# A four-block kernel: the scan's last chunks in an order of their own, and the key weights brought forward in attention

## What is computed

```python
x = x + attn(layernorm(x), wq, wk, wv, wo)
x = x + ffn(layernorm(x), ...)
x = x + mixer(layernorm(x), in_proj_w, conv_w, ..., out_proj_w)
x = x + ffn(layernorm(x), ...)
# mixer, after projection, convolution and silu:
Y_diag = einsum('bcln,bcsn,bhcls,bcshp->bclhp', Cm, Bm, exp(segsum(A)), x)
Y_off  = einsum('bcln,bchpn,bhcl->bclhp', Cm, states, exp(A_cumsum))
y = Y_diag + Y_off + xs * D
g = y * silu(z)
g = g * rsqrt(mean(g * g) + 1e-5) * norm_w
out = g @ out_proj_w.T
```

## Time and profile before

| | us |
|---|---|
| median of 3 runs | 529.23 (528.64 to 529.54) |
| profiled execution | 529.58 |
| its span, first to last instruction | 527.8 |
| TensorE busy | 506.1 (96% of the span) |
| VectorE busy | 410.0 (78%) |
| ScalarE busy | 312.7 (59%) |
| GpSimd busy | 145.7 (28%) |
| mean granted TensorE clock, share of full speed | 0.997 |

### The profile page before, as it was taken

One profiled execution on the slowest core, in us unless ns is written; L12 is line 12 of the kernel. 1 busy time (PEld: TensorE's weight loads), 2 busy tenths in 40 slices (PEclk: granted clock), 3 DMA queues, 4 the chain that ended last, 5 costly groups with the idle time before them and its releaser, 6 DMA issues.

```text
span 527.8 us, 9002 instructions
## 1 busy us (share of the span) xinstructions
PE 506.1 (96%) x2939; PEld 427.1 (81%) x2939; DVE 410.0 (78%) x900; ACT 312.7 (59%) x783; POOL 145.7 (28%) x285
## 2 busy tenths in 40 slices
PE   5999999999999999999999999989988999999996
PEld 4778899999999987678888888758877768888884
DVE  5626567667675898899998999965886779899777
ACT  3656878688687754665443445998762355443342
POOL 2241425344243320110110302379434120020110
PEclk9999999999999999999999999999999999999999
DMA  7320100000001303000040000000000000000101
GB/s 281 105 95 1 36 7 2 2 0 2 2 2 25 131 2 140 6 1 0 1 140 1 2 0 1 1 1 2 0 2 0 1 1 1 1 0 1 40 2 40
DMA packets 5789, 14.23 MB, mean 27 GB/s; under 512 B 624, under 2 KB 2928, under 8 KB 5744
## 3 DMA queue, kind: packets, MB, share of 16 engines
q1 hardware_dynamic: 5744, 13.67, 7.4%
HBM read 12.62 MB, written 1.05 MB: 26 GB/s over the span
## 4 chain that ended last, share of the span: by engine, by line
PE 67%; DVE 19%; issue 6%; ACT 5%; POOL 2%; DMA 1%; DVEq 0%; ACTq 0%; POOLq 0%
PE psum L172 55%; PE psum L475 4%; DVE xs L1973 2%; PE psum L507 2%; DVE ln_stats L212 2%; DVE f_t L1296 1%; DVE xn L232 1%; PE psum L240 1%; DVE f_ch L1365 1%; DVE f_ch_hl L1379 1%; DVE xT_hl L254 1%; POOL ln_rstd L226 1%; DVE f_mix L1374 1%; ACT f_sil L1182 1%; PE psum L468 1%
## 5 line engine op out<-in xcount | busy, mean ns | idle before, releaser
L172 PE MATMUL psum<-xT_hl,ffn_w_hl 128*128 128x512 f32 x312 | 77.7, 396 | 0.9 <-ACT f_sil L1182 0.6
L172 PE MATMUL psum<-f_um,ffn_w_hl 128*128 128x512 f32 x288 | 72.9, 399 | 1.1 <-DVE f_t L1296 0.6
L172 PEld LDWEIGHTS psum<-xT_hl,ffn_w_hl 128*128 128x128 f32 x312 | 56.4, 189 | 13.3 <-DVE ffn_w_hl L897 1.4
L172 PEld LDWEIGHTS psum<-f_um,ffn_w_hl 128*128 128x128 f32 x288 | 53.1, 188 | 15.0 <-DVE f_um L1308 1.7
L1182 ACT ACTIVATE f_sil<-psum 128x512 f32<-128x512 f32 (+1 forms) x48 | 28.1, 596 | 48.8 <-PE psum L172 48.8
L1206 ACT ACTIVATE f_ch_hl<-f_ch 128x512 fp32r<-128x512 f32 x48 | 30.4, 632 | 42.2 <-DVE f_ch L1365 40.5
L172 PE MATMUL psum<-xT_hl,wq_hl 128*128 128x512 f32 x192 | 52.0, 407 | 0.6 <-ACT qT L574 0.6
L172 PE MATMUL psum<-wo_hl,oT_hl 128*128 128x256 f32 x384 | 50.8, 281 | 1.0 <-DVE oT_hl L707 0.6
L172 PEld LDWEIGHTS psum<-wo_hl,oT_hl 128*128 128x128 f32 x384 | 47.8, 188 | 3.7 <-DVE oT_hl L707 1.1
L574 ACT ACTIVATE qT<-psum 128x512 f32<-128x512 f32 x32 | 35.3, 1104 | 22.5 <-PE psum L172 22.4
L583 ACT ACTIVATE probs<-probs,small 120x66 f32<-120x66 f32 x120 | 39.8, 338 | 8.2 <-DVE small L684 8.2
(11 more groups left out here) (265 smaller groups left out, 1152.4 us busy)
## 6 DMA issues: line engine op xcount, KB each, us to landing
w_raw<-in_wq SPq DMA_DIRECT2D x4, 512.0 KB, 4.4
w_raw<-in_wo SPq DMA_DIRECT2D x4, 512.0 KB, 3.3
ffn_w_raw<-in_ffn SPq DMA_DIRECT2D x3, 576.0 KB, 4.9
ffn_w_raw_far<-in_ffn SPq DMA_DIRECT2D x3, 576.0 KB, 5.0
ssd_w_raw<-in_ssd SPq DMA_DIRECT2D x3, 512.0 KB, 5.4
x_resid<-in_x SPq DMA_DIRECT2D x2, 512.0 KB, 4.5
out_x<-x_resid SPq DMA_DIRECT2D x4, 256.0 KB, 2.1
w_raw<-in_wk SPq DMA_DIRECT2D x1, 512.0 KB, 6.6
```

What stands on the lines that cost most here:

```text
L172: i = e.matmul(dst, lhs(a), rhs(b), start=start and n == 0, stop=stop and n == len(TERMS) - 1, **kw)
```

## The change

In attention, SP transfers the identity alone (64 KB) behind x's first half, then wk, then x's second half; the other constants come last, and one unused constant is dropped. ACT splits wk in two halves ahead of the high part of half 0; DVE subtracts wk's first half right behind the norm of half 0 and the second behind the low part; the statistics of half 1 move behind that. TensorE's filler becomes 7 products of 128 columns ahead of the transposes and 4 behind them; it no longer waits for the high parts in between, and the first group of keys waits for each bank's low part alone.

In every layer norm the transposes into bank 0 are done before those into bank 1 (after the first tile), and ACT starts on bank 0 when that is full; DVE's low part waits for all transposes.

In the scan, the loop over DVE's work ends with chunk 6's turn, and what is left is written out in an order of its own; POOL likewise. Chunks 6 and 7 have own buffers for the gated rows' parts, and chunk 5 is no longer folded. TensorE's and ACT's orders are the same.

```diff
+        TR_ORDER = [(0, 0), (0, 1)] + [(i, 0) for i in range(1, HT)] + [(i, 1) for i in range(1, HT)]
...
             def hi_act(e, h):
-                need(e, "tr", h + 1)
                 for k in range(KB):
+                    need(e, "tr", KB * h + k + 1)
...
+                    if n == 0:
+                        x_in(e, 1)
                     if n == 3:
                         e.dma_start(cb_bits[:, :], ins["cb"]).then_inc(s_cb, 16)
                         e.dma_start(par[:, :], ins["par"]).then_inc(s_par, 16)
+                        e.dma_start(cf[:, P:], ins["cf"][:, P:]).then_inc(s_par, 16)
...
-                        e.matmul(bank(7)[:, 0:2 * P], ident, cf[:, 0:2 * P], start=True, stop=True)
+                        e.matmul(bank(7)[:, 0:P], ident, ident, start=True, stop=True)
...
-                e.wait_ge(s_cf, 16)
-                keep_busy(2)
+                e.wait_ge(s_id, 16)
+                keep_busy(7)
                 ln["tr"](e, 0)
-                keep_busy(2)
-                e.wait_ge(LN["hi"], 1)
-                keep_busy(2)
-                e.wait_ge(LN["hi"], 2)
-                keep_busy(2)
-                ln["ready"](e, 0)
+                keep_busy(4)
...
             def act(e):
+                wk_hi(e, 0)
+                wk_hi(e, 1)
                 ln["hi"](e, 0)
-                w_hi(e, 0)
...
                 ln["norm"](e, 0)
+                wk_lo(e, 0)
+                ln["lo"](e, 0)
+                wk_lo(e, 1)
                 ln["stats"](e, *range(HT, NT))
                 ln["veps"](e, 1)
-                ln["lo"](e, 0)
-                wk_lo(e, 0)
-                wk_lo(e, 1)
+                keys_out(0, 0)
                 ln["norm"](e, 1)
-                keys_out(0, 0)
                 ln["lo"](e, 1)
...
-            FOLDED = range(1, NT - 2)
+            FOLDED = range(1, NT - 3)
...
+                mean_square(NT - 5)
+                mix(NT - 1)
+                mean_square(NT - 4)
+                final(NT - 5)
+                split(NT - 3)
+                with_skip(NT - 2)
+                final(NT - 4)
+                new_state(NT - 2)
+                early(phase, "stats", e, NT - 5)
+                early(phase, "veps0", e)
+                split(NT - 2)
+                early(phase, "stats", e, NT - 4)
+                mean_square(NT - 3)
+                early(phase, "norm0", e, (0,))
+                with_skip(NT - 1)
+                final(NT - 3)
+                early(phase, "norm0", e, (1, 2, 3))
+                split(NT - 1)
+                mean_square(NT - 2)
+                early(phase, "lo0", e)
+                early(phase, "stats", e, NT - 3)
+                final(NT - 2)
+                early(phase, "stats", e, NT - 2)
+                mean_square(NT - 1)
+                final(NT - 1)
+                early(phase, "stats", e, NT - 1)
+                early(phase, "logits_copy0", e)
...
+                inverse_rms(NT - 5)
+                inverse_rms(NT - 4)
+                gate(NT - 2)
+                early(phase, "rstd0", e)
+                inverse_rms(NT - 3)
+                gate(NT - 1)
+                inverse_rms(NT - 2)
+                inverse_rms(NT - 1)
```

More of the change, by code:

```diff
@@ L75 @@
 INP_COLS = INNER + INNER + 2 * P
-C_ID, C_AFTER, C_UPTO, C_ONES = (P * i for i in range(4))
+C_ID, C_UPTO, C_ONES = (P * i for i in range(3))
 B_ID, B_ECOL, B_M0 = 0, P, 2 * P
@@ L236, in tr_pe @@
                 banks_free(e, h)
-                for i in range(HT):
+                for i, k in TR_ORDER:
                     need(e, "xn", HT * h + i + 1)
[L239 to L242, removed]
+                    m = e.transpose(bank(banks[h][k])[:, i * P:(i + 1) * P],
+                                    xn(HT * h + i)[:, k * P:(k + 1) * P], ident)
+                    if i == HT - 1:
+                        m.then_inc(LN["tr"], 1)
             def hi_act(e, h):
-                need(e, "tr", h + 1)
                 for k in range(KB):
+                    need(e, "tr", KB * h + k + 1)
                     e.activation(xT[:, HI, k, HALF * h:HALF * h + HALF], bank(banks[h][k]),
@@ L250, in lo_dve @@
             def lo_dve(e, h):
+                need(e, "tr", KB * (h + 1))
                 for k in range(KB):
@@ L2001, in dve @@
                 conv((7, 1), (6, 3), (7, 2), (8, 1), (7, 3), (8, 2), (9, 1), (8, 3), (9, 2), (9, 3))
-                for i in range(NT + 4):
-                    if i >= 4:
[L2004 to L2017, removed]
-                    if i >= 4:
[L2019 to L2056, removed]
-                                        ALU.add).then_inc(S["y"], 1)
-                    if i == NT + 3:
-                        early(phase, "logits_copy0", e)
-                    if i == NT:
-                        early(phase, "norm0", e)
-                    if i == NT + 1:
-                        early(phase, "lo0", e)
@@ new lines, in final, with split @@
+                def final(c):
+                    e.wait_ge(S["ri"], c + 1)
+                    e.scalar_tensor_tensor(out=x[:, c, :], in0=bank(6 + c % 2)[:, 0:D], scalar=RI[:, c:c + 1],
+                                           in1=x[:, c, :], op0=ALU.mult, op1=ALU.add).then_inc(S["fin"], 1)
+                def split(c):
+                    e.wait_ge(S["ghi"], c + 1)
+                    if c in LAST:
+                        e.wait_ge(S["xdd"], c)
+                    e.tensor_tensor(g_part(c, LO), gy[c % 2], f32(g_part(c, HI)), ALU.subtract).then_inc(S["glo"], 1)
+                    if c in FOLDED:
+                        e.wait_ge(S["g2"], c + 1)
+                        if c >= 2:
+                            e.wait_ge(S["ss"], c - 1)
+                        e.tensor_reduce(g2s[:, c % 2, :], g2[c % 2].rearrange("p h l -> p l h"), AX.X,
+                                        ALU.add).then_inc(S["gs"], 1)
@@ new lines, in new_state @@
+                def new_state(c):
+                    new = st[(c + 1) % 2]
+                    e.wait_ge(S["St"], c + 1)
+                    add = bank(5).rearrange("p (h l) -> p h l", h=NH)
+                    if c:
+                        e.wait_ge(S["st1"], c)
+                        e.wait_ge(S["Y"], c)
+                        e.tensor_tensor(new, add, st_t, ALU.add).then_inc(S["st"], 1)
+                    else:
+                        e.tensor_copy(new, add).then_inc(S["st"], 1)
@@ new lines, in with_skip @@
+                def with_skip(c):
+                    e.wait_ge(S["Y"], c + 1)
+                    if c >= 2:
+                        e.wait_ge(S["glo"], c - 1)
+                        e.wait_ge(S["g2"], c - 1)
+                    e.wait_ge(S["xd"], (NH - 1) * (1 if c < HT else 2))
+                    e.wait_ge(S["xda"], 1 if c < HT else 2)
+                    e.tensor_tensor(gy[c % 2], bank(4).rearrange("p (h l) -> p h l", h=NH), xsD[:, :, tile(c)],
+                                    ALU.add).then_inc(S["y"], 1)
@@ new lines, in dve @@
+                for i in range(NT - 1):
+                    if i >= 4:
+                        mean_square(i - 4)
+                    mix(i)
+                    if i >= 4:
+                        final(i - 4)
+                        early(phase, "stats", e, i - 4)
+                    if i >= 2:
+                        split(i - 2)
+                    if i >= 1:
+                        new_state(i - 1)
+                        with_skip(i - 1)
+                mean_square(NT - 5)
+                mix(NT - 1)
@@ new lines, in gate @@
+                def gate(c):
+                    e.wait_ge(S["y"], c + 1)
+                    e.tensor_tensor(gy[c % 2], gy[c % 2], zs[:, :, tile(c)], ALU.mult).then_inc(S["g"], 1)
+                for c in range(NT - 1):
+                    if c >= 4:
+                        inverse_rms(c - 4)
+                    select(c + 1)
+                    e.wait_ge(S["X"], c + 1)
+                    e.wait_ge(S["L"], 2 * c + 1)
+                    if c >= 2:
+                        e.wait_ge(S["St"], c - 1)
+                    e.tensor_tensor(xdd[c % 2], xd[c % 2], Lm[c % 2][:, :, P - 1:P].broadcast_to([P, NH, P]),
+                                    ALU.mult).then_inc(S["xdd"], 1)
@@ L2214, in _ @@
         def _(e):
-            for h in range(2):
-                rows = ins["x"][HALF * h:HALF * h + HALF, :].rearrange("(t p) d -> p t d", p=P)
-                e.dma_start(x[:, HT * h:HT * h + HT, :], rows).then_inc(s_x[h], 16)
-                if h == 0:
-                    e.dma_start(cf, ins["cf"]).then_inc(s_cf, 16)
+            x_in(e, 0)
+            e.dma_start(ident, ins["cf"][:, C_ID:C_ID + P]).then_inc(s_id, 16)
             for ph in chain:
```

100 lines of the change are left out of this document (55 added, 45 removed).

## The result

The changed kernel takes 522.09 us (median of 4 runs, 522.01 to 522.18) against 529.38 (528.64 to 529.82): a ratio of 0.9864, with an interval of 0.9849 to 0.9879, so 7.3 us less. The forecast was 522.4, with a range of 521.0 to 524.8. Its profiled execution took 522.12 us, of which the span is 520.3.

A forecast was written before the change was run, and what follows sets the result against it. The prediction took TensorE, busy for 506.1 of 527.8 us, to bound the kernel. From 529.58 it took off 5.3 for the scan's end and 1.9 for the start, giving 522.4 us, range 521.0 to 524.8.

The forecast's parts named there:

- The sum of TensorE's work: Scan's end, chunk 6's outputs to the logits' transposes: 14.05 us of work without a wait, 5.3 us earlier.
- the term of the unfolded sum of squares: Scan's end: an unfolded projection takes 1.72 + 1.05 - 0.35 = 2.4 us, three of them in the sum.
- the forecast places: Scan's end: times for DVE's and POOL's steps, such as chunk 5's split at about 392.2, before the start's gain.
- the cover: Scan's end: DVE's last steps end near 406.6, needed at 407.3; 0.7 us spare, beyond which each us costs one.
- The clock: Scan's end: no fall of TensorE's granted clock expected; the rival that it falls once, 524.1 us, had chance 0.12.
- The price of the fall: Scan's end: TensorE time lost to the lower clock over 4 us, put at 1.7 us.
- DVE blocked by POOL's powers: Rival, scan's end: POOL's small powers hold up DVE, 1.0 us lost, 523.4 us; chance 0.14.
- The start: Keys begin at about 11.1, not 12.78, those of half 1 at 18.2 against 20.09: 1.9 us earlier.
- the filler behind the transposes: Start: four products on TensorE, ending at 11.8 at the worst and holding the keys for 0.7 us, covered by a later wait.
- wk's landing: Start: wk lands at 6.5, bounds 5.5 to 8.4; rival, as late as before, 523.2 us, chance 0.06.
- half 1's chain: Start: statistics behind wk's second half put half 1's transposes' end at 16.7; TensorE waits about 0.7 us.
- the filler as a risk: Start: less filler may leave TensorE's clock low and the kernel slower, up to 532.9 us; chance 0.03.

The follow-up runs named there:

- e5: The changed kernel with chunk 5 folded on DVE again, in the new order: 522.42 us.
- e6: The changed kernel with one own buffer, for chunk 7 alone, so chunk 6's high part waits for chunk 5's projection again: 522.51 us.
- e4: The kernel before with unread filler products where TensorE waits ahead of the projections of chunks 5, 6 and 7: 529.13 us against 529.55.
- e8: The changed kernel with DVE's statistics of half 1 ahead of the second half of wk: 521.80 us.
- e7: The changed kernel with POOL's power of chunk 4 behind chunk 6's gate again: 523.82 us.
- e11: The changed kernel without the 11 filler products of the start: 523.75 us.
- e9: The changed kernel with x's second half and all later transfers issued only when wk has landed: 521.82 us against 529.54, a single profiled run.
- e10: The changed kernel with x's second half transferred ahead of wk again: 522.88 us.
- e12: The changed kernel with both halves of wk subtracted on DVE ahead of the low part of half 0: 521.39 us.

## Why the prediction was right

**The scan.** The sum of TensorE's work was 14.05 us; from the end of chunk 6's state (390.12 + 1.02) to the mark at 404.83 it is 13.7. By the chain above, the three projections took 7.0 instead of 7.2: the term of the unfolded sum of squares was mis-sized, as its 1.05 contains an end that overlaps the next product, and 0.8 was what it cost. Outputs took 1.8 instead of 1.95 and logits with the low-rank part 3.7 instead of 3.9, for the same reason; the transposes 1.3 instead of 1.0. Together that is 0.4 more gain than the 5.3 of the sum, and so the 5.7.

**DVE and POOL** kept up as worked out. With the 2.1 us of the start taken off, the forecast places were 390.1 for chunk 5's split, 390.7 for chunk 6's skip, 391.3 for chunk 4's `fin` and 398.4 for the last normalised rows; the rows show 389.98, 390.58, 391.18 and 398.13. The copy of the logits ends at 404.57, forecast 404.5. Only the cover was wrong: it is 0.26 us, not 0.7, since TensorE is faster than the sum. e5 and e6 show how thin it is: delays of about 1 us on DVE came through as 0.5. By these rows DVE nearly shares the bound here, and a faster TensorE would gain little; no run tried that.

**The clock** stayed at 1.00, as forecast. The price of the fall was given as 1.7; e4 shows 1.3 of it in the stretch of one execution and nothing clear of noise end to end, so the 1.7 is neither confirmed nor refuted.

**DVE blocked by POOL's powers** was a rival, and it fell. Chunk 6's split ran 393.32 to 394.01 in 0.69 while the norm's power ran from 393.15 to 394.17. The forecast said that the trace of before shows no overlap with a power, and that was a misreading: rows 7 has one (the power at 10.72 beside the low part at 10.50, one of whose inputs is in PSUM, neither lengthened), and further on there is one beside a DVE instruction with both inputs in SBUF, which keeps its usual 0.69:

```profile
292.34 1.03 POOL L226 TENSOR_TENSOR ln_rstd<-ln_var_eps,minus_half 128x4 f32<-128x4 f32 x1 [9.00 <-DVE ln_var_eps L219]
...
292.94 0.69 DVE L1365 TENSOR_TENSOR f_ch<-f_t,f_wb 128x512 f32<-128x512 f32 x1
```

So the rival could have been set lower than 0.14 beforehand. The gate, in contrast, held the norm as the forecast had assumed: three tiles took 1.85 beside it, the longest 1.21, where one took 0.40 ahead of it. The other way round POOL does suffer: where DVE's subtraction had begun about 0.23 earlier, the power took 1.32 (e8) and 1.33 (e7), not 1.01. The Trainium skill (SBUF — State Buffer, "Who interferes with whom") says that the engine that issues first holds the shared ports and the other is fully blocked. The gate's rows come near that; where a power was first, the subtraction was not held, and the measurement decides.

**The start** was forecast at 1.9 and gave 2.0. Keys came at 10.79, not 11.1: the forecast let them wait for both low parts, which end at 11.24, but the first group waits for bank 0's alone. They begin 0.84 behind the start of that low part (9.95), as they do in e11 without any filler (9.86 and 10.69); so the filler behind the transposes, 1.06 in all, held nothing, where I had it end at 11.8 at the worst. Half 1's statistics came at 11.75 and its transposes ended near 16.7, both to the tenth. The mis-sized term was wk's landing: 6.5 by my estimate, 8.08 by the row (inside its bounds of 5.5 to 8.4), since I weighed only the bytes ahead of it; by e9 those behind it count for 1.7 us. It did no harm, as ACT was done with wk at 9.23, and the high part's place had been 9.2. e10 shows the other side of that edge: one transfer more ahead, and 0.8 is gone. That wk fell on the cheap side of it was luck, as the estimate of 6.5 had 1.6 us of cover and the row has none. SP has one extra issue, not two, and it delays nothing: its next one comes at 11.86 instead of 13.26.

**Where the total was lucky.** A gain of 7.2 was forecast and 7.3 came, but by parts that offset each other: the scan gave 0.4 more than its sum and the start 0.1 more, 0.2 went back at the second half's logits, which the forecast does not mention, and the forecast began at the profiled 529.58, 0.2 above the median.

**What the forecast passed over.** It took DVE's new order in the start as given; half 1's chain was named as late next, with a wait of about 0.7 (measured 0.5), but that wk's second half could leave this chain was not drawn from it. e12 got 0.7 from there. And it counted the filler as a risk only; by e11 1.7 of the gain hang on it.

**Open.** Why the kernel before spreads over 1 us from run to run and the changed one over 0.2, no run here settles. e4's start (filler at 3.93 instead of 3.23 us, keys 0.27 later) shows one way in which executions of the old start differ.

## What to carry to other kernels

Where two engines take turns at the end of a loop, write the tail's order out: add up the bound engine's own work from a fixed mark, then place each small instruction of the others by who waits for it; one power of 0.55 us behind a gate cost 1.7 (e7). A wait that is left over names the next edit: look at what stands ahead of its last releaser and can run in that engine's idle time (e12). Check a price that hangs on cover at its edge, in both directions, before calling it free.

## What the runs showed of the hardware

- A transfer's landing depends on what is issued behind it: 512 KB of wk took 4.6 us with nothing behind it (e9, one execution), 6.3 with its followers issued at once (after), though only 576 KB stood ahead in both.
- POOL's power over 4 columns takes 1.01 to 1.04, and 1.32 to 1.33 when a DVE subtraction with both inputs in SBUF has begun 0.23 before it (e7, e8). Beside a subtraction with one input in PSUM it keeps its 1.02; and when the power runs first, the DVE instruction with both inputs in SBUF keeps its 0.69 (before and after).
- Without filler the first keys ran at the pace of 1.2 GHz from 10.69 to about 16.4 (e11), while the granted clock of these stretches reads 1.00. In the start the level was seen in the products' distance alone, not in that number.
